# Two small layer-norm steps and a row flag's product moved from VectorE to GpSimd, one step dropped, and every engine's list drawn anew

## The chip, the cores and the metric

The program runs on one core of a Trainium2 chip. The metric is the device time of one execution in microseconds (us). The core has four computing engines that run side by side, each through its own list of instructions in order: TensorE (PE in the rows; its weight loads are PEld), VectorE (DVE), ScalarE (ACT) and GpSimd (POOL). SyncE (SP) only issues DMA transfers here. An instruction that must follow one on another engine waits on a semaphore, and everything behind it in its own list waits too.

## The reference

The input `x` is 128 samples of 128 nodes with 256 features, and `adj` is one 128 x 128 adjacency matrix. Four graph layers follow one another, and each adds to its own input:

```
h = relu((x - mean(x)) / sqrt(var(x) + 1e-5))       # over the 256 features
x = x + layer_i(h)                                   # i = 0, 1, 2, 3
```

Layer 0 multiplies `h` by two 256 x 256 halves of a weight and sums one product over neighbours. Layer 1 is an attention with one head, whose logits are the sum of one number of the row node and one of the column node, through a leaky relu, masked by `adj`; a row without a neighbour gives zero. Layer 2 is the same with 128 features. Layer 3 has eight heads with queries, keys and values, a masked softmax and an output product.

## The kernel before, in words

The 128 samples go in 64 pairs. A pair passes through 33 tasks of TensorE and some 60 of the other engines, and the kernel is a software pipeline over pairs: at step `t` each engine runs down its own fixed list (its function `step`), and operation `name` there works on pair `p = t - LAG[name]`. So one step does one pair's worth of work, spread over up to twelve pairs. The table `LAG` and the order of the `if due(...)` lines are the whole schedule. The lists were written by a planner, and nothing is reordered on the chip. The table `BANKS` gives each TensorE task its PSUM bank (eight banks); `bank_free` makes a task wait for the copy that last read this bank.

Names that matter below, for layer `i`:

- `stats{i}`, `mv{i}` (VectorE, L456, L465): row sums of `x`, then mean and variance. `veps{i}` (L472) adds eps to the variance, and L473 right behind it makes `nm{i}`, the negative mean. `rstd{i}` (GpSimd, L311) takes the power -0.5, `y{i}` (GpSimd, L319) computes `(x + nm) * rstd`.
- `h{i}t` (TensorE, L886) transposes `y` in four pieces, `h{i}t_hi` (ScalarE, L706) and `h{i}t_lo` (VectorE, L501) take it out as a high and a low part; `ht2` (L724) is the single copy for layer 2.
- `m0`, `m1`, `mj_hi`, `mj_lo`, `t0`, `s0`, `x1`: layer 0. `wh0_mm`, `wh1_mm` and the copies `wh0`, `wh1` (ScalarE, L718): the projections of layer 1. `hh_mm` and `hh` (L730): the projection of layer 2.
- For layers 1 and 2 the column numbers must be spread over all partitions. GpSimd gathers two columns (`dst1`, `dst2`, L342), SyncE writes them to device memory (`row_out`, L252), reads them back spread (`row_in`, L258), and ScalarE forms the logits (`z1`, `z2`, L744). The first four and the last five pairs use a transpose on TensorE instead (L933). Then come `nmax` (mask and maximum, VectorE L511), `exp` (ScalarE L753), `rsum` (VectorE L519), `e1t`, `e2t` (transposes, L941), `at1`, `at2` (copies, L761), `x2_mm`, `x3_mm` (L949) and `x2`, `x3` (VectorE). In layer 1 the reciprocal is also multiplied by a flag that is zero for a row without neighbours: `rsum1`, L524.
- Layer 3: `kt_mm`, `qt_mm`, `v_mm`, then `scores` (L986) into four banks, `nmax3_0` to `nmax3_3` (VectorE L559, four tiles each), `exp3_0` to `exp3_3` (ScalarE L775, four tiles each), `rsum3` (L567), `p3` (GpSimd L348), `pt` (L994), `p3t` (L783), `ot_mm` (L1006), `ot_hi` (L789), `ot_lo` (L573), `x4_mm`, `x4` (L582), then the store.

Of the kernel before, what the change touches and what calls it, by code (L numbers as in the profile page):

```python
# [16 lines left out]
G = 2  # L17
# [30 lines left out]
    "wh0": (1, "wh0_mm", ('wh0',)),
    "v": (0, "v_mm", ('v',)),
    "prepa": (3, "adj_spread", ('adj_rows',)),  # L50
    "pt3": (1, "pt3", ('p3t_3',)),
    "x2b": (5, "x2_mm", ('x2',)),
    "pt1": (6, "pt1", ('p3t_1',)),
    "x1b": (3, "s0", ('x1',)),
    "d2": (2, "d2", ('z2',)),
    "prep": (5, "products", ('w1_split',)),
    "h3t": (1, "h3t", ('h3t_lo',)),
    "pt2": (0, "pt2", ('p3t_2',)),
    "m1": (4, "m1", ('mj_lo1', 't0_1')),
    "x4b": (3, "x4_mm", ('x4',)),  # L60
    "m0": (0, "m0", ('mj_lo0', 't0_0')),
    "kt": (1, "kt_mm", ('kt',)),
    "qt": (5, "qt_mm", ('qt',)),
    "d1": (3, "d1", ('z1',)),
# [1 line left out]
    "at2": (6, "e2t", ('at2',)),
    "ot": (0, "ot_mm", ('ot_lo',)),
    "sc0": (3, "scores", ('nmax3_0',)),
    "sc1": (5, "scores", ('nmax3_1',)),
    "sc2": (4, "scores", ('nmax3_2',)),  # L70
    "sc3": (1, "scores", ('nmax3_3',)),
    "h2t": (6, "h2t", ('ht2',)),
    "x3b": (0, "x3_mm", ('x3',)),
    "wh1": (2, "wh1_mm", ('wh1',)),
# [10 lines left out]
def gnn_kernel(nc, x, adj, w0t, bias0, w1, w1t, a1, w2, w2t, a2, wqt, bq, wkt, bk, wvt, bv, wot, bo, out):  # L85
# [7 lines left out]
    with ExitStack() as ctx:  # L93
# [142 lines left out]
        def _(sp):  # L236
# [23 lines left out]
            def step(t):  # L260
                if due(t, "row_in1") and not at_an_end(t - LAG["row_in1"]):
# [7 lines left out]
                if due(t, "row_out1") and not at_an_end(t - LAG["row_out1"]):  # L269
                    write_row(1, t - LAG["row_out1"])  # L270
                if due(t, "row_in2") and not at_an_end(t - LAG["row_in2"]):
                    spread_row(2, t - LAG["row_in2"])
# [18 lines left out]
        def _(pool):  # L291
# [65 lines left out]
            def step(t):  # L357
                if due(t, "x3_tail"):
                    x3_tail(t - LAG["x3_tail"])
                if due(t, "y0"):  # L360
# [1 line left out]
                if t == LAG["w3_low1"]:
                    low_w3(1)
                if t == LAG["w3_low0"]:
                    low_w3(0)
                if due(t, "r0"):
                    biased_x0(t - LAG["r0"])
                if t == LAG["w3_low2"]:
                    low_w3(2)
                if due(t, "dst2") and not at_an_end(t - LAG["dst2"]):  # L370
                    gather_dst(2, hh, "hh", "hh", F1 + 1, t - LAG["dst2"])
                if due(t, "p3_2"):
                    normalise_p3(2, t - LAG["p3_2"])
                if due(t, "rstd3"):
                    inverse_deviation(3, t - LAG["rstd3"])
                if t == LAG["deg_b_made"]:
                    prepare_deg_b()
                if due(t, "y3"):
                    normalise(3, x3, t - LAG["y3"])
                if due(t, "dst1") and not at_an_end(t - LAG["dst1"]):  # L380
                    gather_dst(1, wh, "wh", last_of("wh0", "wh1"), D + 1, t - LAG["dst1"])
                if due(t, "p3_3"):
                    normalise_p3(3, t - LAG["p3_3"])
# [728 lines left out]
```

## Time and profile before

| what | value |
|---|---|
| time, median of 3 runs | 1276.25 us (1275.59 to 1278.63) |
| the profiled execution: its time, its span | 1276.93 us, 1275.1 us |
| TensorE busy | 1232.8 us, 97% of the span |
| VectorE busy | 1141.8 us, 90% |
| ScalarE busy | 1058.2 us, 83% |
| GpSimd busy | 944.5 us, 74% |
| granted TensorE clock, mean | 0.995 of full |
| idle time of TensorE in 0 to 30, 30 to 60, 60 to 100 us | 15.1, 6.0, 4.9 us |
| busy time of TensorE in 500 to 700 us | 199.79 us of 200 |
| busy time of TensorE in 1245 to 1275 us | 21.2 us of 30 |

Busy time counts what an engine's records cover; records of neighbouring instructions overlap a little. Positions in the rows are microseconds from the span's start. A name of several instructions in a timeline row covers them all: its first number is the start of the first.

### The profile page before, as it was taken

How to read it: one execution, taken by the hardware profiler on the slowest of the kernel's cores; microseconds unless marked ns; L12 is line 12 of the kernel's file. 1: busy time of each engine (PE TensorE's matmuls, PEld its weight loads, DVE VectorE, ACT ScalarE, POOL GpSimd, SP SyncE). 2: the span in 40 equal slices, each digit the busy share in tenths (PEclk: the TensorE clock that was granted, in tenths of full speed). 3: DMA queues.
4: the chain of work that ended last, by engine and by line, in shares of the span. 5: the costliest groups of instructions: out<-in, count | busy, mean ns of one | idle time of the engine just before them, and what ended most of it. 6: DMA issues, size and time to landing. Idle time of an engine off the chain costs nothing. (4 is left out here: it accounts for less than half of the span.)

```text
span 1275.1 us, 43341 instructions
## 1 busy us (share of the span) xinstructions
PE 1232.8 (97%) x12213; PEld 1134.8 (89%) x12213; DVE 1141.8 (90%) x5713; ACT 1058.2 (83%) x3911; POOL 944.5 (74%) x1338
## 2 busy tenths in 40 slices
PE   5799999999999999999999999999999999999997
PEld 4689999999999999999999998999999999999986
DVE  4689999989999999999999999999999999998874
ACT  2468898888888888888889888888889888888886
POOL 4568877877777877777787787777787777787663
PEclk9899999999999999999999999999999999999999
DMA  4011222222112122222112122222122122211001
GB/s 119 24 22 21 38 44 50 37 44 51 36 44 52 36 44 52 36 43 52 38 40 52 40 45 46 41 39 52 40 47 43 41 46 44 43 39 31 18 19 34
DMA packets 70586, 53.57 MB, mean 42 GB/s; under 512 B 20688, under 2 KB 70352, under 8 KB 70352
## 3 DMA queue, kind: packets, MB, share of 16 engines
q1 hardware_dynamic: 68144, 49.35, 19.2%
q8 instruction: 104, 1.70, 0.6%
q14 instruction: 130, 1.06, 0.5%
q10 hardware_dynamic: 2208, 1.45, 0.4%
HBM read 33.89 MB, written 16.89 MB: 40 GB/s over the span
## 5 line engine op out<-in xcount | busy, mean ns | idle before, releaser
L775 ACT ACTIVATE exps<-masked,nmax 128x128 f32<-128x128 f32 x1024 | 397.1, 394 | 0.0
L348 POOL TENSOR_TENSOR probs<-exps,rsum 128x512 f32<-128x512 f32 x256 | 266.7, 1042 | 162.6 <-DVE rsum L567 161.9
L319 POOL TENSOR_SCALAR y<-x,nm,rstd 128x256 f32<-128x256 f32 x512 | 282.8, 563 | 22.5 <-issue 21.0
L311 POOL TENSOR_TENSOR rstd<-veps,power 128x2 f32<-128x2 f32 x256 | 178.2, 696 | 114.4 <-DVE veps L472 109.3
L559 DVE CUSTOM_DVE_ANT_0 masked<-bank,mask 128x128 f32<-128x128 f32 x1024 | 232.0, 280 | 1.3 <-PE bank L986 0.8
L775 ACT ACTIVATION_READ_ACCUMULATOR exps<-masked,nmax 128x1 f32 x1024 | 198.4, 194 | 0.0
L876 PE MATMUL bank<-w_hi,ht_hi 128*128 128x512 f32 (+1 forms) x512 | 192.6, 376 | 4.5 <-DVE ht_lo L501 4.5
L456 DVE BATCH_NORM_STATS2 stats<-x 128x6 f32<-128x256 f32 x512 | 183.9, 411 | 0.2
L886 PE MATMUL bank<-ident,y 128*128 128x128 f32 x1024 | 159.0, 278 | 20.0 <-POOL y L319 19.3
L877 PE MATMUL bank<-w_lo,ht_hi 128*128 128x512 f32 (+1 forms) x512 | 175.4, 343 | 0.0
L878 PE MATMUL bank<-w_hi,ht_lo 128*128 128x512 f32 (+1 forms) x512 | 174.8, 341 | 0.0
L994 PE MATMUL bank<-ident,probs 128*128 128x128 f32 x1024 | 152.8, 272 | 2.2 <-POOL probs L348 1.7
L886 PEld LDWEIGHTS bank<-ident,y 128*128 128x128 f32 x1024 | 119.1, 142 | 36.8 <-issue 12.6
L783 ACT ACTIVATE probs3t<-bank 128x512 f32<-128x512 f32 x256 | 144.0, 591 | 4.0 <-PE bank L994 3.9
L501 DVE SCALAR_TENSOR_TENSOR ht_lo<-bank,ht_hi 128x512 fp32r<-128x512 f32 x192 | 130.8, 681 | 12.2 <-ACT ht_hi L706 12.1
L994 PEld LDWEIGHTS bank<-ident,probs 128*128 128x128 f32 x1024 | 121.2, 141 | 9.3 <-POOL probs L348 2.3
L706 ACT ACTIVATE ht_hi<-bank 128x512 fp32r<-128x512 f32 x192 | 113.6, 592 | 8.1 <-PE bank L886 7.5
L876 PEld LDWEIGHTS bank<-w_hi,ht_hi 128*128 128x128 f32 x512 | 98.5, 192 | 13.0 <-DVE ht_lo L501 5.8
L878 PEld LDWEIGHTS bank<-w_hi,ht_lo 128*128 128x128 f32 x512 | 98.2, 192 | 12.0
L877 PEld LDWEIGHTS bank<-w_lo,ht_hi 128*128 128x128 f32 x512 | 99.1, 194 | 6.3
L753 ACT ACTIVATE ez<-z,nmax 128x128 f32<-128x128 f32 x256 | 99.8, 395 | 1.9 <-DVE nmax L511 1.9
L718 ACT ACTIVATE wh<-bank 128x258 f32<-128x258 f32 x128 | 49.5, 387 | 54.3 <-PE bank L878 50.3
(120 smaller groups left out, 3693.4 us busy)
## 6 DMA issues: line engine op xcount, KB each, us to landing
x<-in_x SPq DMA_DIRECT2D x64, 256.0 KB, 4.6
out<-x SPq DMA_DIRECT2D x64, 256.0 KB, 4.7
db<-rows SPq DMA_DIRECT2D x110, 128.0 KB, 4.1
rows<-dst SPq DMA_DIRECT2D x110, 1.0 KB, 3.0
probs<-in_w0t SPq DMA_DIRECT2D x1, 512.0 KB, 7.9
probs<-in_w1t ACTq DMA_DIRECT2D x1, 256.0 KB, 5.9
exps<-in_wot SPq DMA_DIRECT2D x1, 256.0 KB, 7.6
w_sb<-in_w ACTq DMA_DIRECT2D x1, 256.0 KB, 7.8
```

The lines of the kernel that those rows point to most:

```text
L311: pool.tensor_tensor(rstd[i][:, b], veps[i][:, b], power[:], ALU.pow).then_inc(S[f"rstd{i}"], 1)
L319: last = pool.tensor_scalar(y[i][:, b, g], src[:, bx, g], nm[i][:, s, g:g + 1], rstd[i][:, s, g:g + 1], ALU.add, ALU.mult)
L348: pool.tensor_tensor(probs3[:, p % BUFFERS["probs3"], j], exps3[:, p % BUFFERS["exps3"], j], rsum3[:, s, j].unsqueeze(2).to_broadcast([P, ...
L456: last = dve.bn_stats(stats[i][:, b, g], src[:, bx, g])
L559: last = dve.tensor_tensor_reduce(masked3[:, b, j, i], bank_of(f"sc{j}")[:, i * P:(i + 1) * P], mask[:], scale=-1.0, scalar=-MASKED, op0=A ...
L775: last = act.activation(exps3[:, b, j, i], masked3[:, p % BUFFERS["masked3"], j, i], ACT.Exp, bias=nmax3[:, s, j, i:i + 1], scale=-1.0, ac ...
L783: act.activation(probs3t[:, b, j].rearrange("p b n -> p (b n)"), bank_of(f"pt{j}")[:], ACT.Copy).then_inc(S[f"p3t_{j}"], 1)
L876: pe.matmul(out_ap, lhs[0], rhs[0], start=start, stop=False)
L877: pe.matmul(out_ap, lhs[0], rhs[1], start=False, stop=False)
L878: return pe.matmul(out_ap, lhs[1], rhs[0], start=False, stop=stop)
L886: last = pe.transpose(bank_of(f"h{i}t")[:, (c * G + g) * P:(c * G + g + 1) * P], y[i][:, b, g, c * P:(c + 1) * P], ident[:])
L994: last = pe.transpose(bank_of(f"pt{j}")[:, i * P:(i + 1) * P], probs3[:, p % BUFFERS["probs3"], j, i], ident[:])
```

## The change

The variance plus eps is computed by GpSimd instead of VectorE. The negative mean is no longer made: `normalise` subtracts the mean itself, straight from `mv`. The product with the flag in layer 1 goes to GpSimd as well. `mean_and_variance` now waits until `y` of four pairs ago has read `mv`. All lists, lags and banks are those of a new drawing by the planner.

```diff
@@ gpsimd
+            def shifted_variance(i, p):
+                b = p % SMALL
+                passed(pool, f"mv{i}", p)
+                passed(pool, f"rstd{i}", p, SMALL)
+                pool.tensor_scalar(veps[i][:, b], mv[i][:, b, :, 1], LN_EPS, None, ALU.add).then_inc(S[f"veps{i}"], 1)
+
+            def clear_empty_rows(p):
+                s = p % SMALL
+                passed(pool, "rsum1_any", p)
+                pool.tensor_tensor(rsum[1][:, s], rsum[1][:, s], has_any[:].to_broadcast([P, G]), ALU.mult).then_inc(S["rsum1"], 1)
...
-                passed(pool, f"nm{i}", p)
+                passed(pool, f"mv{i}", p)
                 passed(pool, f"rstd{i}", p)
...
-                    last = pool.tensor_scalar(y[i][:, b, g], src[:, bx, g], nm[i][:, s, g:g + 1], rstd[i][:, s, g:g + 1], ALU.add, ALU.mult)
+                    last = pool.tensor_scalar(y[i][:, b, g], src[:, bx, g], mv[i][:, s, g, 0:1], rstd[i][:, s, g:g + 1], ALU.subtract, ALU.mult)
@@ vector
                 passed(dve, f"veps{i}", p, SMALL)
-                passed(dve, f"nm{i}", p, SMALL)
+                passed(dve, f"y{i}", p, SMALL)
...
-            def shifted_variance(i, p):
-                b = p % SMALL
-                passed(dve, f"mv{i}", p)
-                passed(dve, f"y{i}", p, SMALL)
-                dve.tensor_scalar(veps[i][:, b], mv[i][:, b, :, 1], LN_EPS, None, ALU.add).then_inc(S[f"veps{i}"], 1)
-                dve.tensor_scalar(nm[i][:, b], mv[i][:, b, :, 0], -1.0, None, ALU.mult).then_inc(S[f"nm{i}"], 1)
...
-            def clear_empty_rows(p):
```

The new lists, with the pair in brackets where it matters (`t` is the step), setup lines left out:

```
SP    row_in2(t-3) row_out1(t-1) row_in1(t-1) load(t+3) row_out2(t-2) store(t-7)
   was row_in1(t) load(t+4) row_out2(t-1) store(t-7) row_out1(t+1) row_in2(t-1)
PE    h0t pt1 pt2 pt0 x2_mm pt3 s0 x4_mm m0 h3t d2 m1 v_mm kt_mm qt_mm e2t d1 h1t ot_mm scores h2t x3_mm wh0_mm wh1_mm hh_mm e1t
   was e1t h0t pt0 wh0_mm v_mm pt3 x2_mm pt1 s0 d2 h3t pt2 m1 x4_mm m0 kt_mm qt_mm d1 h1t e2t ot_mm scores h2t x3_mm wh1_mm hh_mm
ACT   h1t_hi ot_hi exp1 ht2 exp3_1 wh0 wh1 hh at1 h0t_hi p3t_1 p3t_2 exp3_0 exp3_2 h3t_hi p3t_3 mj_hi0 z2 p3t_0 v mj_hi1 exp2 exp3_3 at2 z1
DVE   stats3 stats0 mv3 nmax3_2 h0t_lo nmax3_3 x2 x1 rsum3_0 mv0 stats1 x4 mv1 h3t_lo stats2 nmax2 mv2 rsum3_1 mj_lo0 t0_0 mj_lo1 kt t0_1
      rsum3_2 qt rsum2 nmax1 h1t_lo rsum3_3 ot_lo nmax3_1 rsum1_any x3 nmax3_0
POOL  p3_3 dst1 rsum1 dst2 veps3 rstd3 y3 r0 p3_0 veps0 r3 veps1 rstd1 veps2 y1 rstd2 y2 rstd0 p3_1 p3_2 y0 x3_tail
```

Of the banks, `h0t`, `m0`, `ot` and `wh0` now share bank 3; `pt1`, `pt3`, `qt`, the scores' second bank and `wh1` share bank 4; `pt0`, `h1t`, `x3b` and `at1` share bank 2. Before, `ot` and `x3b` shared bank 0.

## Rows read from the trace of the kernel before

**Rows 1.** The page, part 1: busy time and share of the span of each engine.
```profile
PE 1232.8 (97%) x12213; PEld 1134.8 (89%) x12213; DVE 1141.8 (90%) x5713; ACT 1058.2 (83%) x3911; POOL 944.5 (74%) x1338
```

**Rows 2.** Timeline of TensorE, one step: start, duration, instruction.
```profile
601.20 0.40 PE L876 MATMUL bank<-w_hi,ht_hi 128*128 128x512 f32 x1
...
602.59 0.28 PE L876 MATMUL bank<-ht_hi,wk_hi 128*128 128x256 f32 x1
...
611.16 0.60 PE L886 MATMUL bank<-ident,y 128*128 128x128 f32 x4
...
611.96 0.36 PE L876 MATMUL bank<-w_hi,ht_hi 128*128 128x258 f32 x1
...
612.76 0.28 PE L876 MATMUL bank<-wv_hi,ht_hi 128*128 128x256 f32 x1
...
620.08 0.40 PE L876 MATMUL bank<-w_hi,ht_hi 128*128 128x512 f32 x1
```

**Rows 3.** Timeline of SyncE's queue: the first and last steady row_out2, and one step.
```profile
156.52 0.32 SPq L252 DMA_DIRECT2D rows<-dst  x1
...
611.81 0.32 SPq L252 DMA_DIRECT2D rows<-dst  x1
...
615.97 1.91 SPq L258 DMA_DIRECT2D db<-rows  x2
...
1144.46 0.32 SPq L252 DMA_DIRECT2D rows<-dst  x1
```

**Rows 4.** Waits, whole span: who waited for whom, total us, times, longest.
```profile
ACT bank L744 <- DMA db<-rows: 38.6, 49, 2.0
```

**Rows 5.** Timeline of VectorE in a step with a late row: start, duration, instruction.
```profile
342.28 0.69 DVE L501 SCALAR_TENSOR_TENSOR ht_lo<-bank,ht_hi 128x512 fp32r<-128x512 f32 x1
...
343.02 0.69 DVE L573 TENSOR_TENSOR ot_lo<-bank,ot_hi 128x512 fp32r<-128x512 f32 x1
343.63 0.28 DVE L559 CUSTOM_DVE_ANT_0 masked<-bank,mask 128x128 f32<-128x128 f32 x1
...
344.58 0.61 DVE L542 SCALAR_TENSOR_TENSOR x<-bank,rsum,x 128x128 f32<-128x128 f32 x2
```

**Rows 6.** Timeline of TensorE in that step; in brackets the idle time before.
```profile
343.86 0.68 PE L949 MATMUL bank<-hh,at 128*128 128x128 f32 x4 [0.58 <-DVE ot_lo L573]
```

**Rows 7.** Instruction groups by line: busy us, mean ns, idle before.
```profile
L472 DVE TENSOR_SCALAR veps<-mv 128x2 f32<-128x2 f32 x256 | 81.8, 324 | 0.2
L342 POOL COPY dst<-hh 128x2 f32<-128x2 f32 x55 | 10.5, 191 | 11.6 <-ACT hh L730 10.2
```

**Rows 8.** Timelines of VectorE and of GpSimd at one moment.
```profile
611.77 1.02 DVE L472 TENSOR_SCALAR veps<-mv 128x2 f32<-128x2 f32 x1
...
611.73 1.04 POOL L348 TENSOR_TENSOR probs<-exps,rsum 128x512 f32<-128x512 f32 x1
```

**Rows 9.** Timeline of ScalarE: start, duration, instruction.
```profile
605.89 0.68 ACT L744 ACTIVATE bank<-db,wh 128x128 f32<-128x128 f32 x2
606.51 0.58 ACT L706 ACTIVATE ht_hi<-bank 128x512 fp32r<-128x512 f32 x1
606.99 0.37 ACT L761 ACTIVATE at<-bank 128x256 f32<-128x256 f32 x1
607.35 0.60 ACT L789 ACTIVATE ot_hi<-bank 128x512 fp32r<-128x512 f32 x1
...
612.96 0.39 ACT L718 ACTIVATE wh<-bank 128x258 f32<-128x258 f32 x1
613.24 0.39 ACT L775 ACTIVATE exps<-masked,nmax 128x128 f32<-128x128 f32 x1
...
614.78 0.58 ACT L767 ACTIVATE v<-bank 128x512 f32<-128x512 f32 x1
```

**Rows 10.** The tiles dst and db: DMA to landing in us, min/median/max.
```profile
DMA to landing us min/median/max: 2.5/3.0/4.7
...
DMA to landing us min/median/max: 2.9/4.1/5.4
```

More of the change, by code:

```diff
@@ L29 @@
 LAG = {
[11 rows of a table removed]
[11 rows of a table added]
 }
 BANKS = {
-    "at1": (0, "e1t", ('at1',)),
-    "h0t": (6, "h0t", ('h0t_lo',)),
+    "h0t": (3, "h0t", ('h0t_lo',)),
+    "pt1": (4, "pt1", ('p3t_1',)),
+    "pt2": (6, "pt2", ('p3t_2',)),
     "pt0": (2, "pt0", ('p3t_0',)),
[L48 to L64, printed above, removed]
-    "h1t": (2, "h1t", ('h1t_lo',)),
[L66 to L74, printed above, removed]
+    "x2b": (1, "x2_mm", ('x2',)),
+    "pt3": (4, "pt3", ('p3t_3',)),
+    "x1b": (5, "s0", ('x1',)),
+    "x4b": (6, "x4_mm", ('x4',)),
+    "prep": (4, "products", ('w1_split',)),
+    "m0": (3, "m0", ('mj_lo0', 't0_0')),
+    "h3t": (0, "h3t", ('h3t_lo',)),
+    "d2": (1, "d2", ('z2',)),
+    "m1": (6, "m1", ('mj_lo1', 't0_1')),
+    "v": (5, "v_mm", ('v',)),
+    "kt": (0, "kt_mm", ('kt',)),
+    "qt": (4, "qt_mm", ('qt',)),
+    "at2": (1, "e2t", ('at2',)),
+    "d1": (0, "d1", ('z1',)),
+    "prepa": (2, "adj_spread", ('adj_rows',)),
+    "h1t": (2, "h1t", ('h1t_lo',)),
+    "ot": (3, "ot_mm", ('ot_lo',)),
+    "sc0": (6, "scores", ('nmax3_0',)),
+    "sc1": (4, "scores", ('nmax3_1',)),
+    "sc2": (5, "scores", ('nmax3_2',)),
+    "sc3": (0, "scores", ('nmax3_3',)),
+    "h2t": (1, "h2t", ('ht2',)),
+    "x3b": (2, "x3_mm", ('x3',)),
+    "wh0": (3, "wh0_mm", ('wh0',)),
+    "wh1": (4, "wh1_mm", ('wh1',)),
     "hh": (1, "hh_mm", ('hh',)),
+    "at1": (2, "e1t", ('at1',)),
     "zz2": (7, "z2", ('nmax2',)),
@@ L186, in gnn_kernel @@
         x_out = [sem(f"x_out{i}") for i in range(BUFFERS["x4"])]
-        S = {name: sem(name) for name in LAG if name not in ("row_in1", "load", "row_out2", "store", "row_out1", "row_in2")}
-        for name in ("nm0", "nm1", "nm2", "nm3",):
-            S[name] = sem(name)
+        S = {name: sem(name) for name in LAG if name not in ("row_in2", "row_out1", "row_in1", "load", "row_out2", "store")}
         def due(t, operation):
@@ L260, in step @@
             def step(t):
+                if due(t, "row_in2") and not at_an_end(t - LAG["row_in2"]):
+                    spread_row(2, t - LAG["row_in2"])
+                if due(t, "row_out1") and not at_an_end(t - LAG["row_out1"]):
+                    write_row(1, t - LAG["row_out1"])
                 if due(t, "row_in1") and not at_an_end(t - LAG["row_in1"]):
@@ L268, in step @@
                     store(t - LAG["store"])
[L269 to L272, printed above, removed]
             load(0)
@@ L357, in step @@
             def step(t):
+                if due(t, "p3_3"):
+                    normalise_p3(3, t - LAG["p3_3"])
+                if due(t, "dst1") and not at_an_end(t - LAG["dst1"]):
+                    gather_dst(1, wh, "wh", last_of("wh0", "wh1"), D + 1, t - LAG["dst1"])
+                if due(t, "rsum1"):
+                    clear_empty_rows(t - LAG["rsum1"])
+                if due(t, "dst2") and not at_an_end(t - LAG["dst2"]):
+                    gather_dst(2, hh, "hh", "hh", F1 + 1, t - LAG["dst2"])
@@ L362, in step @@
[L362 to L383, printed above, removed]
@@ L519, in inverse_sum @@
                 dve.reciprocal(rsum[i][:, s], ssum[i][:, s]).then_inc(S[name], 1)
-            def clear_empty_rows(p):
-                s = p % SMALL
-                passed(dve, "rsum1_any", p)
-                dve.tensor_tensor(rsum[1][:, s], rsum[1][:, s], has_any[:].to_broadcast([P, G]), ALU.mult).then_inc(S["rsum1"], 1)
             def sum_x2(p):
@@ L791, in step @@
             def step(t):
+                if due(t, "h1t_hi"):
+                    relu_transposed_high(1, ht1_r, last_of("wh0_mm", "wh1_mm"), t - LAG["h1t_hi"])
+                if due(t, "ot_hi"):
+                    high_ot(t - LAG["ot_hi"])
+                if due(t, "exp1"):
+                    exps(1, "rsum1_any", t - LAG["exp1"])
+                if due(t, "ht2"):
+                    relu_transposed2(t - LAG["ht2"])
+                if due(t, "exp3_1"):
+                    exps3_of(1, t - LAG["exp3_1"])
+                if due(t, "wh0"):
+                    copy_projection1(0, t - LAG["wh0"])
                 if due(t, "wh1"):
@@ L832, in step @@
                 if due(t, "z1"):
                     sum_logits(1, wh, "wh", D, t - LAG["z1"])
-                if due(t, "h1t_hi"):
-                    relu_transposed_high(1, ht1_r, last_of("wh0_mm", "wh1_mm"), t - LAG["h1t_hi"])
-                if due(t, "at2"):
-                    copy_exp_transposed(2, t - LAG["at2"])
-                if t == LAG["w0_high"]:
-                    round_w0()
-                if due(t, "ot_hi"):
-                    high_ot(t - LAG["ot_hi"])
-                if due(t, "exp1"):
-                    exps(1, "rsum1_any", t - LAG["exp1"])
@@ L1073, in step @@
                     attend(2, hh, "hh", F1, t - LAG["x3_mm"])
+                if due(t, "wh0_mm"):
+                    project1(0, t - LAG["wh0_mm"])
                 if due(t, "wh1_mm"):
```

311 lines of the change are left out of this document (160 added, 151 removed), and 22 rows, old and new, of the table LAG.

## The prediction

> **What bounds the kernel now.** I read the busy shares first, then TensorE's timeline over one step, then the waits, then the timelines of the others around each wait. TensorE is busy 97% of the span [rows 1], and in mid-run it never stops: the first product of layer 0 begins at 601.20 and again at 620.08, so a step of unbroken TensorE work lasts 18.88 us [rows 2]. 64 such steps make 1208 us of a span of 1275; the other 67 us are fill, drain and lost time. The lost part of the steady stretch can be read off SyncE's row_out2, issued once a step: 156.52 to 1144.46 is 987.94 us over 52 steps, 19.00 us each [rows 3], 0.12 us more than the unbroken step, 6.2 us in all. Its cause is the detour of layer 2's row through device memory. ScalarE waits for it in 49 of 55 steps, 38.6 us together, up to 2.0 us [rows 4]. What is late there runs on through ScalarE's list to ot_hi, to ot_lo on VectorE, and since ot and x3b share a bank, x3_mm stalls: 0.58 us behind ot_lo in such a step, which ends at 343.71 and releases TensorE at 343.86 [rows 5, 6]. VectorE itself is no bound. So the change can win at most these 6.2 us plus something at the ends, unless it creates a new wait.
>
> **The change, part by part.** On VectorE it removes four veps, four nm and one flag product a step. The veps rows average 0.324 us, 81.8 us in all [rows 7], though an undisturbed one takes 0.16: one of them lasts 1.02 us whenever it starts 0.04 us after a GpSimd product of 1.04 us, and it ends with that product [rows 8]. At a pitch of about 0.07 us for eight of the nine, plus this 0.9 us, VectorE gets back 1.4 us of 18.88. TensorE doesn't wait for that engine's load, so I cost this at nothing; the bounds are 0 and the 6.2 us of lost time.
>
> On GpSimd it adds four veps and one flag product a step. The trace has no such instruction on this engine. The nearest row, a copy of the same 128x2, takes 0.19 us [rows 7]; from below it can't be under zero, from above the whole 128x512 product gives 1.04 [rows 8]. With 0.19 and about 0.1 of waiting for itself, five make 1.5 us; GpSimd is idle for 26% of a step, 4.9 us [rows 1], and in the new list it waits for VectorE's mv3 and mv2 anyway. At 1.04 each they would make 5.2, more than the idle time, 0.3 a step or 17 us. I take 0.19, as the nearest shape.
>
> One of them has a place that matters: rsum1 stands between dst1 and dst2, so row_out2 leaves some 0.2 us later. Against that, row_in2 no longer stands behind row_out1: before, it went out 4.16 us after row_out2 in the step shown [rows 3], though a row lands after a median of 3.0 [rows 10]. I set these two against each other.
>
> The Trainium skill (Perfetto Trace Analysis, Optimizing GPSIMD Operations) advises other engines where possible, since GpSimd is generally slower; rows 7 show 0.19 us for its small copy against 0.16 for VectorE's small instruction, so here the rule is weak for 128x2, but it is the reason why rsum1 at a higher price is one of the rivals.
>
> TensorE's own work doesn't change in kind or number; only neighbours do, and I keep 18.88.
>
> The new lists decide the rest. I lay them on TensorE's line with h0t at 0 and walk the tightest ring. The old run from the first product of kt (602.59) to h0t (611.16) is 8.57 us [rows 2]. In the new list it also holds wh0_mm: 0.80 by the rows (611.96 to 612.76), of which I leave out 0.08 for the switch from a transpose, since wh1_mm, of the same kind, now follows it directly. So kt begins 9.29 us before the next h0t (9.37 with the switch). h0t writes bank 3 and must wait for the copy wh0. That copy hangs on v_mm's end, the start of kt, thus: v's copy starts 0.20 later (612.76 to 612.96 is such a step [rows 2, 9]); v 0.48, mj_hi1 0.28, exp2 0.77 (half of four tiles), exp3_3 1.54, at2 0.36, z1 0.62, and h1t_hi until its end 0.58 [rows 9]: 4.83. On VectorE h1t_lo and rsum3_3 0.74 (342.28 to 343.02), ot_lo 0.61, nmax3_1 0.92, with 0.03 before [rows 5]: 2.30, at 7.13. On ScalarE, after a release of about 0.1, exp3_1 1.54 and wh0 until its end 0.39 [rows 9], and 0.15 until TensorE goes [rows 5, 6]: 9.31. The ring is 9.31 against 9.29. So it closes to within my reading: I book 0.05 us a step for it, with minus 0.15 to plus 0.3 as its bounds.
>
> z2 comes in this ring ahead of v. Laid out the same way ScalarE is free for it at 8.1 after h0t and may start up to 8.69 before v's copy is late. The row was ready 0.7 us behind its slot on average before (38.6 over 55 [rows 4]), which in the new line is 8.3. With its spread of about half a microsecond the overshoot is 0.06 a step. Together 0.11 times 52 is 5.7 us, in place of 6.2.
>
> z1: row_out1 goes out right after row_in2, at 4.5, row_in1 behind its landing (3.0), db lands 4.1 later [rows 10]: 11.8, against a slot at 13.2. I cost it at nothing; ScalarE's 1.4 us of margin cover it.
>
> At the start, veps0 of pair 0 is on the path to the first transpose: plus 0.3. The first three steps' y1 now stands behind veps2, thus behind mv2, but x1 and stats1 come sooner as veps and nm are gone; zero. In the drain exp3, p3 and copies of the last pair keep their number, zero, give or take 1.
>
> **Sum.** 1276.9 (the profiled execution: span 1275.1 and 1.8 around it) - 6.2 + 5.7 + 0.3 = 1276.7. That execution lay 0.7 above the median, so the median should be 1276.0.
>
> **The rivals.** (A) The ring has room: my releases are too long by 0.1 or 0.2, the late row costs nothing more, and the 6.2 us are gone but for 1: 1276.0 - 5 is 1271. For it: TensorE waits for ot_lo only in rows like that of [rows 6], and ot and x3b are now in different banks. Against it: the ring just laid out.
>
> (B) The ring is too long, slower than before: each 0.1 us of it costs 5.2 us. With 0.25 a step, 13 us, and the late rows on top: 1276 - 6 + 13 + 3, 1286. It decides from a ring of 9.29 + 0.12, above which it costs more than what is lost now. For it: seven handovers between engines lie in it, two of them booked by guess.
>
> (C) The row of layer 1 is late. Its write now stands behind the read of row 2, whose 128 KB it must share the engines with, and its own read comes after. With both at their longest (4.7 and 5.4 [rows 10]) z1 is ready at 14.7, 1.5 late. If it is late on average by 0.5, 27 us: 1300.
>
> (D) rsum1 on GpSimd costs 0.7 rather than 0.2: the row 0.5 later, z2 ready at 8.8 on average, 0.3 a step, 10 us more: 1286. The rule named above speaks for this one; the copy of 0.19 against it.
>
> That the instructions don't move is excluded: they are written out.
>
> **How the numbers follow.** My forecast 0.40, (A) 0.28, (B) 0.18, (C) 0.06, (D) 0.08. A measurement of this kernel tells about 0.3%, 3.8 us, from no change. (A) is faster by over that, and a tenth of the forecast's own cases too: 0.32. (B), (C), (D) are slower, and 0.04 of the forecast's: 0.36 and the rest, 0.32, within. The range from 1268 to 1288 leaves out (C) and the far ends.
>
> **What would show it.** Right: row_out2 every 18.95 to 19.0 us; VectorE's busy time down by some 130 us, with no small instruction at 1 us; TensorE's waits in mid-run at h0t behind ACT wh, not at x3_mm behind ot_lo; GpSimd's veps near 0.19. (A): steps of 18.87 to 18.90. (B): h0t waiting in every step. (C): ScalarE waiting for the DMA of db ahead of bank<-db,wh. (D): rsum<-rsum,has_any on GpSimd well over 0.2. I would be wrong at the root if TensorE waited for a y, or if the same TensorE work took another time in its new order.

## The result, and the profile after

The changed kernel takes 1482.7 us (median of 4 runs, 1479.2 to 1485.58) against 1276.64 of the kernel before on the same chip (4 runs): ratio 1.161, 95% interval 1.158 to 1.164. It is 16% slower, 206 us. The forecast was 1276.0, with 1268 to 1288 as its range.

The page of the kernel after, part 1, and the costliest group of its part 5 (operation, count | busy us, mean ns of one | idle before):

```profile
PE 1290.6 (87%) x12213; PEld 1141.1 (77%) x12213; DVE 1064.1 (72%) x5137; ACT 1051.8 (71%) x3911; POOL 1344.8 (91%) x1658
...
L327 POOL TENSOR_SCALAR y<-x,mv,rstd 128x256 f32<-128x256 f32 x512 | 624.8, 1229 | 23.1 <-issue 21.7
```

The same group in the kernel before:

```profile
L319 POOL TENSOR_SCALAR y<-x,nm,rstd 128x256 f32<-128x256 f32 x512 | 282.8, 563 | 22.5 <-issue 21.0 <-POOL rstd L311 1.4
```

This is where to look first. Against [rows 1], TensorE fell from 97% to 87% and GpSimd rose from 74% to 91%, 944.5 to 1344.8 us. Of these 400 us the normalisation alone makes 342 (624.8 - 282.8): the same 512 instructions on the same 128x256 elements take 1229 ns instead of 563. What differs is the operand (a column of `mv`, every second number) and the first operation, subtract for add.

The small new instructions of GpSimd, from its groups by line in the kernel after:

```profile
L309 POOL TENSOR_SCALAR veps<-mv 128x2 f32<-128x2 f32 x256 | 57.7, 226 | 74.9 <-DVE mv L483 74.0
...
L314 POOL TENSOR_TENSOR rsum<-rsum,has_any 128x2 f32<-128x2 f32 x64 | 12.9, 201 | 0.0
L350 POOL COPY dst<-wh 128x2 f32<-128x2 f32 x55 | 10.5, 192 | 0.0
```

They cost what [rows 7] let expect, 0.2 us each, so rival (D) is out. The waits of the kernel after over its whole span (who waited for whom: us in total, times, longest):

```profile
PE bank L882 <- POOL y L327: 126.7, 144, 5.2
ACT bank L740 <- DMA db<-rows: 109.4, 103, 4.3
...
PE bank L872 <- DVE x L588: 34.7, 55, 1.0
```

TensorE now waits for `y`, in 144 places, and ScalarE's wait for the rows in device memory is 109.4 us in 103 places, where it was 38.6 in 49 [rows 4]: both layers' rows are late now, and a row's write lands after a median of 4.2 us against 3.0 in [rows 10]. SyncE's queue shows the step. Its first and last lines here are stores:

```profile
163.98 0.43 SPq L242 DMA_DIRECT2D out<-x  x1
...
609.70 0.32 SPq L249 DMA_DIRECT2D rows<-dst  x1
...
614.22 0.32 SPq L255 DMA_DIRECT2D db<-rows  x1
614.63 0.38 SPq L249 DMA_DIRECT2D rows<-dst  x1
618.44 0.32 SPq L255 DMA_DIRECT2D db<-rows  x1
...
631.65 0.32 SPq L249 DMA_DIRECT2D rows<-dst  x1
...
1058.56 0.43 SPq L242 DMA_DIRECT2D out<-x  x1
```

Between the two stores lie 40 steps: 894.58 / 40 = 22.36 us each, against 19.00 in [rows 3]. Over 52 steps the 3.36 us make 175 of the 209 us by which the span grew (1275.1 to 1483.8). 7 us of the rest lie ahead of the first of these rows (the first store of the same stretch stood at 156.89 before), some 27 behind those steps, in the drain.

Which chain of waits sets a step of 22 us? The way to find out is to follow one round through the engines, from each instruction to what released it, until the round closes on itself. Such a closed round is called a ring here: a step can't be shorter than the ring is long. GpSimd, from `veps2` to the copy `dst2`:

```profile
618.55 0.22 POOL L309 TENSOR_SCALAR veps<-mv 128x2 f32<-128x2 f32 x1 [0.20 <-DVE mv L483]
618.75 2.45 POOL L327 TENSOR_SCALAR y<-x,mv,rstd 128x256 f32<-128x256 f32 x2
...
622.04 2.44 POOL L327 TENSOR_SCALAR y<-x,mv,rstd 128x256 f32<-128x256 f32 x2 [0.17 <-issue]
...
627.14 2.43 POOL L327 TENSOR_SCALAR y<-x,mv,rstd 128x256 f32<-128x256 f32 x2
...
631.44 0.18 POOL L350 COPY dst<-hh 128x2 f32<-128x2 f32 x1
```

Then SyncE writes the row (631.65, in the fence above). ScalarE forms the logits when it has been read back, and VectorE masks them, and right behind that takes the next mean and variance, for which `veps2` waits:

```profile
639.80 0.68 ACT L740 ACTIVATE bank<-db,hh 128x128 f32<-128x128 f32 x2 [1.63 <-DMA db<-rows]
```

```profile
640.51 0.29 DVE L522 CUSTOM_DVE_ANT_0 z<-bank,mask 128x128 f32<-128x128 f32 x1 [1.72 <-ACT bank L740]
...
640.94 0.24 DVE L483 BATCH_NORM_AGGREGATE mv<-stats 128x2 f32<-128x6 f32 x2
```

That is a ring: 13.1 us of GpSimd's list, some 8 us for the detour of layer 2's row, 1.5 for the two small pieces, 22.7 in this round. It holds three normalisations, `y1`, `y2` and `y0`; `y3` stands in GpSimd's list outside it. The prediction laid out another ring (v, wh0, h0t) and never this one. GpSimd's own list is close behind: in the 21.96 us from one `dst2` to the next (609.48 to 631.44) it waited 0.20 us for `mv2` and 0.34 for `mv3`. TensorE's waits in and around this step are these:

```profile
607.67 0.66 PE L882 MATMUL bank<-ident,y 128*128 128x128 f32 x4 [1.30 <-POOL y L327]
...
624.53 0.66 PE L882 MATMUL bank<-ident,y 128*128 128x128 f32 x4 [0.39 <-POOL y L327]
629.63 0.66 PE L882 MATMUL bank<-ident,y 128*128 128x128 f32 x4 [0.98 <-POOL y L327]
```

### The profile page after: what moved, and what is told of

Same layout as the page of the kernel before. It is cut to its first block and busy times, and to the rows that moved or that the text cites. A ratio compares the mean times of both kernels' runs of the same rounds, so it can differ in the third digit from the quotient of the medians.

```text
span 1483.8 us, 43088 instructions
## 1 busy us (share of the span) xinstructions
PE 1290.6 (87%) x12213; PEld 1141.1 (77%) x12213; DVE 1064.1 (72%) x5137; ACT 1051.8 (71%) x3911; POOL 1344.8 (91%) x1658
## 5 line engine op out<-in xcount | busy, mean ns | idle before, releaser
L327 POOL TENSOR_SCALAR y<-x,mv,rstd 128x256 f32<-128x256 f32 x512 | 624.8, 1229 | 23.1 <-issue 21.7
L882 PE MATMUL bank<-ident,y 128*128 128x128 f32 x1024 | 166.0, 285 | 127.0 <-POOL y L327 126.7
L882 PEld LDWEIGHTS bank<-ident,y 128*128 128x128 f32 x1024 | 115.4, 142 | 170.6 <-POOL y L327 160.5
L319 POOL TENSOR_TENSOR rstd<-veps,power 128x2 f32<-128x2 f32 x256 | 183.7, 718 | 11.0
L522 DVE CUSTOM_DVE_ANT_0 z<-bank,mask 128x128 f32<-128x128 f32 x256 | 64.2, 289 | 139.8 <-ACT bank L740 139.7
L990 PE MATMUL bank<-ident,probs 128*128 128x128 f32 x1024 | 133.2, 273 | 3.4 <-DVE nmax L565 2.6
L990 PEld LDWEIGHTS bank<-ident,probs 128*128 128x128 f32 x1024 | 117.2, 141 | 11.6 <-issue 3.8
L309 POOL TENSOR_SCALAR veps<-mv 128x2 f32<-128x2 f32 x256 | 57.7, 226 | 74.9 <-DVE mv L483 74.0
```

The costliest lines, as they stand in the source:

```text
L319: pool.tensor_tensor(rstd[i][:, b], veps[i][:, b], power[:], ALU.pow).then_inc(S[f"rstd{i}"], 1)
L327: last = pool.tensor_scalar(y[i][:, b, g], src[:, bx, g], mv[i][:, s, g, 0:1], rstd[i][:, s, g:g + 1], ALU.subtract, ALU.mult)
L882: last = pe.transpose(bank_of(f"h{i}t")[:, (c * G + g) * P:(c * G + g + 1) * P], y[i][:, b, g, c * P:(c + 1) * P], ident[:])
L990: last = pe.transpose(bank_of(f"pt{j}")[:, i * P:(i + 1) * P], probs3[:, p % BUFFERS["probs3"], j, i], ident[:])
```

## The experiments

Ratios are to the kernel before on the same chip, with 95% intervals; the kernel before ran at 1282 to 1287 us on these chips. "Step" is the mean distance of SyncE's stores between the first one behind about 155 us (up to 166, in old_subtract 182) and about 1070 us of the profiled execution, 40 to 48 steps. The 19.00 comes from the first chip, where the kernel before took 1277 us; on the others its nearest stand-in is old_stride, which ran as fast as it. Kernels in the new lists with add and without nm leave out the sign of the mean: they add it where the reference subtracts it. Of the rows with subtract in some layers only, this holds for the other layers. Below, an instruction with subtract is called dear and one with add cheap.

| run | lists | y | row_out1 ahead of row_in2 | ratio | step, us |
|---|---|---|---|---|---|
| before | old | add | yes | 1 | 19.00 |
| after | new | subtract | no | 1.161 | 22.36 |
| old_subtract | old | subtract | yes | 1.124 | 21.69 |
| old_stride | old | add, strided operand | yes | 0.999 | 19.12 |
| old_veps_pool | old | add, veps by GpSimd | yes | 1.002 | 19.17 |
| new_add | new | add | no | 1.048 | 20.40 |
| new_add_sp | new | add | yes | 0.988 | 18.88 |
| new_sub_sp | new | subtract | yes | 1.161 | 22.49 |
| new_half_sp | new | subtract in 1, 2 | yes | 1.095 | 21.10 |
| new_sub03_sp | new | subtract in 0, 3 | yes | 1.034 | 19.81 |
| new_sub3_sp | new | subtract in 3 | yes | 0.993 | 18.98 |
| new_nm_pool_sp | new | add, nm by GpSimd | yes | 0.993 | 18.94 |
| new_nm_dve_sp | new | add, nm by VectorE | yes | 1.023 | 19.64 |
| new_nm_pool | new | add, nm by GpSimd | no | 1.052 | 20.41 |
| new_add_thin | new | add, thin row 2 | no | 0.991 | 19.04 |

**The price of the instruction.** The kernel before with 44 extra instructions behind GpSimd's list, four of each form:

```diff
+            for name, col, width, first, second in (("add_mult", 0, 256, ALU.add, ALU.mult), ("sub_mult", 0, 256, ALU.subtract, ALU.mult),
+                                                    ("mult_add", 0, 256, ALU.mult, ALU.add), ("mult_sub", 0, 256, ALU.mult, ALU.subtract),
+                                                    ("wide", 2, 256, ALU.add, ALU.mult), ("sub_only", 0, 256, ALU.subtract, None),
+                                                    ("min_mult", 0, 256, ALU.min, ALU.mult), ("imm_sub", None, 256, ALU.subtract, ALU.mult),
+                                                    ("add_mult", 0, 128, ALU.add, ALU.mult), ("sub_mult", 0, 128, ALU.subtract, ALU.mult)):
...
+                    pool.tensor_scalar(fd[name][:, 0:width], fs[:, 0:width], one, two, first, *(() if second is None else (second,))).then_inc(forms, 1)
```

> The kernel before with 44 small GpSimd instructions behind its last step, four of each form, on tiles of their own. Theory S (the operator): in a tensor_scalar, subtract as the first operation takes about 1.22 us at 128x256 where add with mult takes 0.56; a subtraction in tensor_tensor form is not concerned. Rival T (the operand): reading the scalar from a column of a wider tile is what is slow; then sub_mult from a packed column takes 0.56 and the forms with scalars from the tile fc are all alike. Rival L (the lists: GpSimd kept waiting inside its instruction by VectorE): both take 0.56 here, where VectorE is idle. If S holds, sub_mult at 128x128 tells whether the extra grows with the width (0.33 more) or is fixed (0.66 more).

Its groups on GpSimd in the last 60 us, different shapes apart:

```profile
L421 POOL TENSOR_SCALAR f_mult_sub<-fs,fc 128x256 f32<-128x256 f32 x4 | 4.9, 1224 | 0.4
L421 POOL TENSOR_SCALAR f_sub_mult<-fs,fc 128x256 f32<-128x256 f32 x4 | 4.9, 1224 | 0.4
L421 POOL TENSOR_SCALAR f_min_mult<-fs,fc 128x256 f32<-128x256 f32 x4 | 4.9, 1218 | 0.4
...
L421 POOL TENSOR_SCALAR f_sub_only<-fs,fc 128x256 f32<-128x256 f32 x4 | 3.7, 925 | 0.4
L421 POOL TENSOR_SCALAR f_sub_mult<-fs,fc 128x128 f32<-128x128 f32 x4 | 3.2, 796 | 0.4
...
L425 POOL TENSOR_TENSOR f_sub_only<-fs 128x256 f32<-128x256 f32 x4 | 2.5, 613 | 0.3
...
L421 POOL TENSOR_SCALAR f_add_mult<-fs,fc 128x256 f32<-128x256 f32 x4 | 2.2, 558 | 0.4
L421 POOL TENSOR_SCALAR f_wide<-fs,fc 128x256 f32<-128x256 f32 x4 | 2.2, 557 | 0.4
L421 POOL TENSOR_SCALAR f_add_mult<-fs,fc 128x128 f32<-128x128 f32 x4 | 1.8, 452 | 0.4
```

Beside a multiply, a subtraction with a scalar makes the instruction 2.2 times as long, whether it comes first or second; so does a minimum (two further forms: mult-add takes 558 ns, subtract-mult with immediate scalars 1072). These are the kernel's own 563 and 1229, though VectorE does next to nothing here (2.1 us from 1269 us on), so rival L is out too. The strided scalar ("wide") costs nothing. From 128 to 256 columns add-mult grows by 0.83 ns a column and subtract-mult by 3.34, so the dear form pays per element. A tensor_tensor subtraction takes 613 ns, so subtracting isn't dear in itself. Why the scalar form is so stays open; no run looks inside the instruction.

**One change in the old kernel.** `nm` holds the mean with its own sign, and `y` subtracts it:

```diff
-                    last = pool.tensor_scalar(y[i][:, b, g], src[:, bx, g], nm[i][:, s, g:g + 1], rstd[i][:, s, g:g + 1], ALU.add, ALU.mult)
+                    last = pool.tensor_scalar(y[i][:, b, g], src[:, bx, g], nm[i][:, s, g:g + 1], rstd[i][:, s, g:g + 1], ALU.subtract, ALU.mult)
...
-                dve.tensor_scalar(nm[i][:, b], mv[i][:, b, :, 0], -1.0, None, ALU.mult).then_inc(S[f"nm{i}"], 1)
+                dve.tensor_scalar(nm[i][:, b], mv[i][:, b, :, 0], 1.0, None, ALU.mult).then_inc(S[f"nm{i}"], 1)
```

> The old lists; L473 makes the positive mean instead of the negative one and y subtracts it. One operator of the 512 y instructions is all that changes on GpSimd. Theory S: y takes 1.23 us instead of 0.56, GpSimd's work grows by 5.3 us a step over 4.2 us of idle time, so the step becomes 20 us or more: 1350 to 1420. Rivals T and L: y stays at 0.56 and the time at 1276.

Measured 1445.6 us, 1.124 (1.122 to 1.127), above the 1350 to 1420 written down, and the group of `y` in its trace:

```profile
L319 POOL TENSOR_SCALAR y<-x,nm,rstd 128x256 f32<-128x256 f32 x512 | 624.2, 1228 | 22.5 <-issue 21.1 <-POOL rstd L311 1.4
```

So one word in the source (and a sign on VectorE that goes with it), with lists, banks and everything else old, costs 12%. The ring that closes its step of 21.69 us wasn't laid out. Its waits from 200 to 1180 us show ScalarE held by a row in each of the 45 steps (89.2 us) and GpSimd by veps (54.0 us).

**The strided operand in the old kernel.** `nm` gets every second column, as `mv` has it:

```diff
-        nm = [sb(f"nm{i}", [P, SMALL, G]) for i in range(4)]
+        nm = [sb(f"nm{i}", [P, SMALL, G, 2]) for i in range(4)]
```

> The old lists; the negative mean is written to and read from every second column of a tile, as the mean lies in mv; add and mult stay. Theory S: y stays at 0.56 us and the time within 0.3% of 1276.6. Rival T: y takes 1.23 us and the time is 1350 to 1420.

Measured 0.999 (0.997 to 1.001), `y` at 564 ns. The operand's form is out.

**The new lists with the old instruction.** The changed kernel with add for subtract:

```diff
-                    last = pool.tensor_scalar(y[i][:, b, g], src[:, bx, g], mv[i][:, s, g, 0:1], rstd[i][:, s, g:g + 1], ALU.subtract, ALU.mult)
+                    last = pool.tensor_scalar(y[i][:, b, g], src[:, bx, g], mv[i][:, s, g, 0:1], rstd[i][:, s, g:g + 1], ALU.add, ALU.mult)
```

> The new lists and everything of the change but the operator: y adds the mean instead of subtracting it, so the values are not those of the reference. Theory S: y falls to 0.56 us and the time to what the new lists are worth, 1266 to 1288, about 1276 by my walk along the ring; the step is 18.9 to 19.1 us. Rivals T and L: y stays at 1.23 us and the time at 1483, since operand and lists are those of the changed kernel.

Measured 1347.9, 1.048 (1.045 to 1.052), outside the 1266 to 1288 written down. So the lists cost something of their own. Waits of ScalarE from 200 to 1180 us, then SyncE's queue in one step:

```profile
ACT bank L740 <- DMA db<-rows: 88.2, 74, 3.4
```

```profile
600.82 0.32 SPq L249 DMA_DIRECT2D rows<-dst  x1
...
605.14 0.32 SPq L255 DMA_DIRECT2D db<-rows  x1
605.55 0.38 SPq L249 DMA_DIRECT2D rows<-dst  x1
610.36 0.32 SPq L255 DMA_DIRECT2D db<-rows  x1
```

Row 1 was ready when row 2 was (dst1 stands ahead of dst2 on GpSimd), but its write goes out at 605.55, 4.7 us later, behind row 2's read, which waits for row 2's landing. Row 1's read waits in turn for the landing of row 1's write and goes out at 610.36, 4.8 us behind the write. Taken one by one, row 1's writes land 5.5 us behind their issue on average (43 steps between 180 and 1080 us), where the prediction put 3.0 [rows 10]. This is rival (C). The late row closes a ring of its own:

```profile
614.60 0.68 ACT L740 ACTIVATE bank<-db,wh 128x128 f32<-128x128 f32 x2 [1.19 <-DMA db<-rows]
619.62 0.63 ACT L714 ACTIVATE wh<-bank 128x258 f32<-128x258 f32 x2
```

```profile
620.31 0.19 POOL L350 COPY dst<-wh 128x2 f32<-128x2 f32 x1 [1.61 <-ACT wh L714]
```

z1 waits for the row, the copies wh stand behind z1 in ScalarE's list, and dst1 waits for wh: 45 times in this kernel from 200 to 1180 us, 71.1 us in all. The dst1 before stood at 600.33, so this round took 19.98 us.

**The order of two DMAs.** The same, and in SyncE's list row_out1 stands ahead of row_in2:

```diff
-                if due(t, "row_in2") and not at_an_end(t - LAG["row_in2"]):
-                    spread_row(2, t - LAG["row_in2"])
                 if due(t, "row_out1") and not at_an_end(t - LAG["row_out1"]):
                     write_row(1, t - LAG["row_out1"])
+                if due(t, "row_in2") and not at_an_end(t - LAG["row_in2"]):
+                    spread_row(2, t - LAG["row_in2"])
```

> As new_add (the mean added instead of subtracted, so the values are not the reference's), and in SyncE's list row_out1 stands before row_in2 instead of behind it. Theory C (the row of layer 1 is late, since its write shares the DMA engines with the 128 KB read issued just before it): row_in1 goes out 3 us after row_out1 instead of 4.7 to 5, ScalarE waits for db in z1 in few steps, the step falls from 20.05 to 18.9 to 19.0 us and the ratio to before from 1.048 to 0.995 to 1.005. Rival B (the ring v - exp3_3 - z1 - h1t - ot_lo - nmax3_1 - exp3_1 - wh0 - h0t is too long by itself): the step stays at 19.5 or more, with TensorE waiting at h0t for the copy wh0.

That is the order in which they stand in the old list. Measured 1268.9, 0.988 (0.984 to 0.991), better than the 0.995 to 1.005 written down. One step of its queue, and the busy time of the engines from 200 to 1180 us:

```profile
609.03 0.32 SPq L249 DMA_DIRECT2D rows<-dst  x1
...
609.92 0.42 SPq L249 DMA_DIRECT2D rows<-dst  x1
612.11 3.08 SPq L255 DMA_DIRECT2D db<-rows  x2
```

```profile
200.00:1180.00 980.00, 979.11 (x9869) 908.33 (x9868) 846.94 (x4146) 849.39 (x3164) 808.00 (x1339) 1.00 0.22 43
```

The columns of the second fence after the window and its length are PE, PEld, DVE, ACT and POOL, then the granted clock. TensorE is busy 979.1 us of 980. The swap alone is worth 79 us (1347.9 to 1268.9), and the new lists are then faster than the old.

What the swap mends is mainly the moment of issue. From row 2's write to row 1's read, all issued by SyncE, new_add takes 9.67 us on average and new_add_sp 6.06 (47 steps). Of these 3.6 us, 3.1 are row 1's write going out earlier. It lands only a little faster, after 4.8 us instead of 5.5; a 256 KB store is now issued 0.5 us ahead of it. So theory C of the text above, by which the 128 KB read made the landing slow, accounts for a small part of what the swap gained.

**The swap in the changed kernel itself** (same diff, subtract kept):

> The changed kernel with the same swap in SyncE's list and nothing else: y subtracts. The two costs, the slow operator and the late row, lie on different engines. If GpSimd's work alone sets the step (theory M, the larger of the two counts), nothing changes: 1.155 to 1.165 of before. If they add up (rival), it falls by the same 60 us, to about 1.11.

Measured 1492.6, 1.161 (1.158 to 1.165): worth nothing there. So the two losses don't add. With add the late row costs 6.0 points; with subtract the ring through GpSimd and row 2 is the longer one and covers it.

**A thin row 2.** As new_add, but row 2 is read back onto 16 partitions instead of 128 from the third row on:

```diff
-                sp.dma_start(db[i][:, b], rows[i][b].rearrange("n g -> (n g)").partition_broadcast(P)).then_inc(row_in[i][b], 16)
+                n = 16 if i == 2 and q >= 2 else P
+                sp.dma_start(db[i][0:n, b], rows[i][b].rearrange("n g -> (n g)").partition_broadcast(n)).then_inc(row_in[i][b], 16)
```

> As new_add (mean added, values not the reference's) in its own list order, row_in2 ahead of row_out1; but from the third row on row_in2 spreads its row over 16 partitions instead of 128, 16 KB instead of 128, and layer 2's logits take old numbers on the rest. If row_out1 lands late because its 1 KB stands behind these 128 KB (sharing), row_in1 goes out 3 to 3.4 us after row_out1 instead of 4.7, and the step falls from 20.05 to 18.9 to 19.3. If only the issue is late (SyncE held at row_in2 until row 2 has landed), row_in1 still goes out 4.5 to 5 us after row_out1 and the step stays at 19.8 to 20.1.

Measured 0.991 (0.989 to 0.994) with row_in2 still ahead of row_out1. Landing times of the row writes (`dst`) in new_add and in this kernel, min/median/max:

```profile
DMA to landing us min/median/max: 2.6/4.6/8.0
```

```profile
DMA to landing us min/median/max: 2.6/3.9/5.5
```

The writes land sooner when the read ahead is small, 0.7 us in the median and 2.5 at the worst. Row 1's write alone lands after 3.9 us on average (47 steps) instead of 5.5: between the two answers written down, while the step of 19.04 is the first one's. It goes out no earlier (4.18 us behind row 2's, 4.16 in new_add), so here row 1 gains by its landing alone: row 2's write to row 1's read is 8.14 us. Both cures fit new_add's ring, by an estimate from these means: the thin read takes 1.5 us out of its 20.40, which leaves 18.9, the swap 3.6, which leaves 16.8, and TensorE's own 18.88 is the floor. But the thin read also lands sooner itself (2.6 us in the median by the list of its transfers, a full one 4.5), so z2 is early too. The run doesn't split the gain between the two rows.

**Half of the dear instructions.** As new_add_sp, with the subtraction in layers 1 and 2:

```diff
+                    last = pool.tensor_scalar(y[i][:, b, g], src[:, bx, g], mv[i][:, s, g, 0:1], rstd[i][:, s, g:g + 1], ALU.add if i in (0, 3) else ALU.subtract, ALU.mult)
```

> As new_add_sp, but layers 1 and 2 subtract and only layers 0 and 3 add the mean (so the values are not the reference's). GpSimd's busy time a step is 15.7 us in new_add_sp and 20.6 in the changed kernel. Theory M (the larger count): 18.2 busy plus about 0.9 of waiting for mv is 19.1 against TensorE's 18.81, so 1.00 to 1.02 of before. Rival (each slow y costs the time wherever it is): half of the way from 0.988 to 1.161, 1.075.

Measured 1408.7, 1.095 (1.091 to 1.100). Both answers written down were too low: half of the dear instructions cost 10.7 points of 17.3. Busy times from 200 to 1180 us:

```profile
200.00:1180.00 980.00, 911.44 (x8818) 812.57 (x8820) 769.96 (x3710) 758.41 (x2830) 848.23 (x1207) 1.00 0.20 40
```

GpSimd works 848 of 980 us there, less than in the next kernels, which are faster. So it isn't its load. The next two forecasts come from a ring drawn in this trace. It isn't quite the one of the section above: behind y1, y2 and y0 it goes on through x3's tail, stats3, x4 and r3. The trace speaks against that way on. GpSimd is through with r3 and still waits 1.03 us for mv2, for which VectorE's mask waited 1.18 on z2, and z2 1.08 on row 2; from 200 to 1180 us ScalarE waits for a row 47 times, once a step. Both rings hold the same three y, so the forecasts are the same by either.

**The other half, and layer 3 alone.** The same line with `ALU.subtract if i in (0, 3)` and `if i in (3,)`:

> The changed kernel with row_out1 ahead of row_in2, and y of layers 0 and 3 with the subtraction, 1 and 2 with an addition: the other half. (Where the mean is added its sign is wrong, so the values are not the reference's.) GpSimd's load is that of new_half_sp to the instruction. Path theory: the steady step is the longer of TensorE's 18.88 us and a ring that passes through y1, y2, y0 and the tail of x3 on GpSimd, then stats3 on VectorE, x4, r3 and back. new_half_sp, with the dear form in two of its three y (4 x 0.67 = 2.7 us), had 20.82; so with three cheap ones the ring is 18.1, 0.7 under TensorE's step, and with y0 dear alone 18.1 + 1.3 = 19.5: 0.6 us a step, some 35 us, a ratio of 1.010 to 1.025. Load theory: equal load on GpSimd costs the same wherever it stands, 1.09 to 1.10.

> The same with the subtraction in y of layer 3 alone (the other three add, so the values are not the reference's). Path theory: y3 stands outside that ring, behind it GpSimd waits for VectorE's rsum3, x4 and mv2 anyway (0.46, 0.23 and 1.0 us in a step of new_half_sp), so the 1.33 us more a step cost nothing: steps of 18.9 us, a ratio of 0.985 to 0.995. Load theory: a quarter of the dear instructions costs about a quarter of what all four cost, 0.988 + 0.043, 1.02 to 1.04.

Measured 1.034 (1.031 to 1.038) and 0.993 (0.991 to 0.996). new_sub03_sp, then new_sub3_sp, same window:

```profile
200.00:1180.00 980.00, 950.18 (x9364) 867.40 (x9363) 811.19 (x3957) 806.95 (x3012) 901.48 (x1286) 1.00 0.22 42
```

```profile
200.00:1180.00 980.00, 978.49 (x9828) 904.73 (x9826) 841.35 (x4114) 842.34 (x3141) 876.11 (x1337) 1.00 0.23 43
```

The same load in other places costs 4.6 points instead of 10.7, and the dear `y3`, outside the ring, costs next to nothing, though GpSimd is then busy 876 us, more than in new_half_sp. The load theory is out. The first run is above its interval, since the ring was taken from one round (18.1 with cheap instructions). The means of the table give it better: a pair of `y` takes 2.44 us dear and 1.09 cheap, 1.35 more. 21.10 less two of them is 18.40, 19.81 less one is 18.46, 22.49 less three is 18.44. Three kernels with two, one and three dear pairs in the ring give one length of it within 0.06 us. At 18.4 it is 0.45 under TensorE's own 18.88; with three dear pairs it becomes 22.5. This tells which y lie in the ring, not by which way it goes on; for that the waits above are the evidence.

**veps alone in the old lists.** Only the eps addition goes to GpSimd, right ahead of rstd; nm stays on VectorE:

> The old lists; veps alone goes to GpSimd, right ahead of rstd; the negative mean stays on VectorE and y adds. Theory P (VectorE's relief is off the path): 0.995 to 1.003 of before. veps takes 0.2 to 0.23 us on GpSimd. The instruction of 1 us a step on VectorE does not go but moves to nm, which is of the same form. Rival: the extra 0.3 us on GpSimd ahead of rstd shows at y, 1.003 to 1.01.

Measured 1.002 (1.000 to 1.004). This part of the change is neither a gain nor a loss there; nm then takes 229 ns on average on VectorE, up to 1082, so the long instruction did move to it.

**Who makes the negative mean.** With add, the mean must change its sign first, so nm comes back. new_nm_pool_sp lets GpSimd make it behind veps, new_nm_dve_sp VectorE behind mv, new_nm_pool is the first with the changed kernel's own DMA order:

```diff
+                passed(pool, f"y{i}", p, SMALL)
+                pool.tensor_scalar(nm[i][:, b], mv[i][:, b, :, 0], -1.0, None, ALU.mult).then_inc(S[f"nm{i}"], 1)
...
-                passed(pool, f"mv{i}", p)
+                passed(pool, f"nm{i}", p)
...
+                    last = pool.tensor_scalar(y[i][:, b, g], src[:, bx, g], nm[i][:, s, g:g + 1], rstd[i][:, s, g:g + 1], ALU.add, ALU.mult)
```

> The new lists with the swap, the negative mean made by GpSimd right behind each veps, y adds it: the reference's values. GpSimd has four small instructions more, 0.2 to 0.3 us each, some 1.1 us a step in all. Theory: it is still under the step, 0.995 to 1.01 of before. Rival: the extra 0.3 ahead of each rstd makes y1 late for h1t; then TensorE waits for y and it is 1.01 to 1.03.

> The new lists with the swap in SyncE's list; the negative mean is made by VectorE right behind each mv (four tensor_scalar a step), veps and the flag's product stay on GpSimd, y adds: the reference's values. VectorE has room (847 of 980 us busy), so 0.985 to 0.995 of before, a little better than with nm on GpSimd (0.993). The nm that starts beside a GpSimd product should last up to 1 us, as in the kernel before. Rival: these stalls lie in the path of mv to y and cost 0.1 us or more a step, 0.995 to 1.005.

> The new lists in their own SyncE order with the negative mean made by GpSimd and y adding: the reference's values. Theory C: the late row is the same as in new_add, step 20.05, 1.045 to 1.055 of before, against 0.993 with the swap. If the swap's gain hung on y adding a wrong mean, it would not appear here.

new_nm_pool_sp measured 1275.4, 0.993 (0.991 to 0.996). It computes what the reference does and is faster than both kernels, a little more than its 0.995 to 1.01 had it. Its new group, on GpSimd:

```profile
L315 POOL TENSOR_SCALAR nm<-mv 128x2 f32<-128x2 f32 x256 | 57.7, 225 | 20.9
```

Four small instructions of 0.23 us a step buy back four pairs at 1.35. new_nm_pool measured 1.052 (1.050 to 1.055): the order of the two DMAs costs 5.9 points in this version.

new_nm_dve_sp measured 1.023 (1.021 to 1.025), where I had expected 0.985 to 0.995. VectorE and GpSimd in one step of it:

```profile
620.51 0.97 DVE L490 TENSOR_SCALAR nm<-mv 128x2 f32<-128x2 f32 x1
...
622.91 1.30 DVE L490 TENSOR_SCALAR nm<-mv 128x2 f32<-128x2 f32 x1
```

```profile
620.42 1.04 POOL L360 TENSOR_TENSOR probs<-exps,rsum 128x512 f32<-128x512 f32 x1 [1.09 <-DVE rsum L579]
...
622.90 1.29 POOL L347 TENSOR_TENSOR r<-x,c 128x512 f32<-128x512 f32 x1 [1.25 <-DVE x L594]
```

Each of these nm, 0.17 us when undisturbed, starts within 0.1 us of a GpSimd product and ends with it (621.48 and 621.46, 624.21 and 624.19). The second product waits for VectorE's x4, which the first nm has made late, and the pair of 0.98 and 1.31 us is there again in the next step (640.11, 642.52): 1.9 us of VectorE's time. Over the run nm takes 608 ns on average. The places and lengths are read; that these two cause the whole 0.7 us by which the step is longer than in new_nm_pool_sp wasn't tested apart.

## Why the prediction was wrong

- **The normalisation's price (the failed step).** The text priced veps, nm and the flag product, and had no term at all for `y`, whose operation changes from add to subtract. It counts 512 times in the trace. It went from 563 to 1229 ns. The bounds of the prediction ended at 1.04 us for a small instruction, while this one sat outside every bound. old_subtract shows that this alone costs 12% in the old lists; in the new ones it makes 17.3 points (new_add_sp 0.988, new_sub_sp 1.161).
- **GpSimd's spare time.** The comparison of 1.5 us of new work with 4.9 idle was right for those instructions (226 and 201 ns), though in the steady stretch GpSimd idled 4.3 us a step and not 4.9 (busy 756.6 of 980 us). But load was the wrong measure: with 5.3 us more for `y` GpSimd still isn't full (91%), and a step is set by a ring in which only three of the four `y` lie. Such a ring has 0.45 us of slack a step, not 4.9.
- **z1 at nothing.** The 3.0 us for the landing of row 1's write was the median of the old order, where the write stood 2.8 us behind the store (3.0 on average there). Right behind row 2's read it took 5.5 on average, 2.5 more than booked against a margin of 1.4. Rival (C) had the mechanism, and its 1300 was too low: 1.048 is some 61 us for it, since z1 sets off a ring through wh and dst1. It had a chance of 0.06. In the changed kernel itself this error cost nothing (new_sub_sp); it would have failed the forecast without the first one.
- **The ring v, wh0, h0t.** Booked at 9.31 against 9.29, a loss of 0.05 a step. In new_add_sp TensorE is busy 979.1 of 980 us and h0t doesn't wait, so (B) is out. With add, and with the two DMAs in their old order, rival (A)'s step of 18.87 to 18.90 comes out: 18.88. The new lists as they were drawn never ran like that.
- **The relief of VectorE.** The 1.4 us a step was right: 17.7 us busy before (913.5 of 980 us), 16.3 in new_add_sp (846.9). The sign of "some 130 us" was not: busy time fell by 77.7, 1141.8 to 1064.1. The 130 is near the sum of the dropped rows' own durations (81.8, 45.6 and 10.1), which overlap their neighbours. No small instruction of 1 us is left there in the changed kernel. That the relief buys nothing by itself fits old_veps_pool (1.002), which moves only veps.
- **The 6.2 us of late rows.** TensorE's own step of 18.88 was right to the hundredth (new_add_sp). As a bound of what can be won 6.2 us was too low on the other chips: new_add_sp is 1.2% faster, some 16 us. The old lists lose more there: old_stride's step is 19.12, and 0.24 us over 52 steps is 12 us. The other 4 weren't traced.

The prediction named as its root failure "if TensorE waited for a y". That is what the trace shows.

The Trainium skill (GPSIMD Engine Reference, Elementwise — side-by-side cycle accounting) says that for up to two operations the body is bound by the ports, "at 1.03 cyc/elem". By that rule subtract and add cost the same. At the 1.2 GHz with which that section reckons, 1.03 cycles are 0.86 ns, an estimate. The trace of forms agrees for add-mult (0.83 ns a column) and not for subtract-mult (3.34 ns a column); the measurement decides.

The Trainium skill's page SBUF — State Buffer (Who interferes with whom) says that a VectorE tensor_scalar, which can enter a two-port mode, and a GpSimd instruction then exclude each other: whoever issues first has the shared pair of ports for the whole instruction, and the other blocks. The trace agrees: nm of 0.97 and 1.30 us in new_nm_dve_sp starts just behind the product beside it and ends with it. Which mode nm ran in no run here shows.

## What to carry to other kernels

Price every instruction whose operation changes, even by a word, and count its instances first: here one word in 512 instructions outweighed a planner's whole redrawing. When an engine's work grows, look for the ring it stands in (follow one round from release to release through all engines and DMAs) and read the slack there, not in its busy share. A small DMA that stands behind a large one in a queue has two prices: the wait of the large one ahead of it, which delays its own issue, and a slower landing. Read both from rows with the same neighbours.

## What the runs showed of the hardware that was not expected

- GpSimd's tensor_scalar with a subtract or a min takes 1218 to 1224 ns at 128x256, with add and mult in either order 558. A lone subtract takes 925, with immediate scalars 1072, a tensor_tensor subtract 613.
- The stride of the scalar operand costs nothing (557 ns).
- How long row 1's write of 1 KB takes to land varied with what was issued ahead of it (means of 43 to 47 steps): 3.0 us with a 256 KB store 2.8 us ahead (before), 3.9 with a 16 KB read 0.4 us ahead (new_add_thin), 4.8 with the store 0.5 us ahead (new_add_sp), 5.5 with a 128 KB read 0.4 us ahead (new_add).
